# Fetching one of 32 gathered row blocks by single-row transfers from SyncE

## What is computed

```python
def _gcn_layer(x, W, b, edge_weight, edge_src, edge_dst):
    support = x @ W
    msgs = support[edge_src] * edge_weight[:, None]
    agg = jax.ops.segment_sum(msgs, edge_dst, num_segments=N_NODES)
    return agg + b
h = jax.nn.elu(_gcn_layer(x, W1, b1, edge_weight, edge_src, edge_dst))
h = jax.nn.elu(_gcn_layer(h, W2, b2, edge_weight, edge_src, edge_dst))
```

## Time and profile before

| | us |
|---|---|
| median of 3 runs (5253.92 to 5268.12) | 5263.27 |
| the profiled execution | 5257.51 |
| its span, first to last instruction | 5255.6 |

### The profile page before, as it was taken

How to read it: one execution, slowest core, us unless ns; L and a number is a source line. 1 busy time by engine, 2 the same in 40 slices (tenths; PEclk the granted TensorE clock), 3 DMA queues, 4 the chain that set the end, 5 groups by cost and what they waited for, 6 DMA issues and landing times. The chain is left out here.

```text
span 5255.6 us, 89454 instructions
## 1 busy us (share of the span) xinstructions
PE 4074.3 (78%) x25266; PEld 3747.3 (71%) x25267; DVE 2650.4 (50%) x9578; ACT 814.5 (15%) x2507; POOL 3445.0 (66%) x3639
## 2 busy tenths in 40 slices
PE   0577777777777777769988999898989987069998
PEld 0467666666667776758888888888888886058886
DVE  7433333333333333355676666767666666234444
ACT  2001111111111111111222222222222222011111
POOL 0577777777777777757777777777777774632222
PEclk9867777777777777778999999999999998589999
DMA  7444444444444444434555454555545553632221
GB/s 212 142 128 132 130 132 132 130 132 130 132 131 133 132 130 132 129 89 125 147 147 152 143 151 145 147 149 146 151 144 148 147 146 109 188 112 70 67 70 65
DMA packets 409075, 693.81 MB, mean 132 GB/s; under 512 B 108237, under 2 KB 275661, under 8 KB 408893
## 3 DMA queue, kind: packets, MB, share of 16 engines
q0 software_dynamic: 177312, 488.43, 32.8%
q1 hardware_dynamic: 195765, 163.17, 10.6%
q10 hardware_dynamic: 35920, 41.25, 2.2%
HBM read 562.84 MB, written 129.68 MB: 132 GB/s over the span
## 5 line engine op out<-in xcount | busy, mean ns | idle before, releaser
L395 PEld LDWEIGHTS sums<-sel,rows 128*128 128x128 f32 x13312 | 1888.7, 222 | 768.0 <-DMA rows<-xn,idx 440.8
L395 PE MATMUL sums<-sel,rows 128*128 128x64 f32 x13312 | 1894.5, 305 | 672.9 <-DMA rows<-xn,idx 354.6
L451 POOL DMA_INDIRECT rows<-xn,idx x1664 | 1577.8, 948 | 642.4 <-issue 630.8
L451 POOL DMA_INDIRECT rows<-h,idx x1664 | 1585.3, 953 | 578.5 <-issue 528.9
L403 DVE TENSOR_SCALAR sel<-cols,rel_now,wgt_now 128x64 f32<-128x64 f32 x3360 | 780.4, 336 | 7.8
L409 DVE TENSOR_TENSOR agg<-agg,sums 128x128 f32 x832 | 240.3, 289 | 783.9 <-issue 604.7
L603 DVE TENSOR_TENSOR pre<-z,b_g 128x256 f32<-128x256 f32 x98 | 41.6, 424 | 526.8 <-PE z L598 526.8
L1807 PE MATMUL y_ps<-w,e_hidden 128*128 128x256 f32 x1248 | 286.1, 389 | 0.0
L1795 PE MATMUL e_hidden_ps<-tokens_t,w 128*128 128x256 f32 x1248 | 279.2, 381 | 4.4 <-DVE e_hidden L1864 3.6
L983 PE MATMUL hidden_ps<-xt,w 128*128 128x128 f32 x1664 | 265.2, 282 | 17.2 <-ACT msg_t L1104 17.0
L1735 POOL DMA_INDIRECT out<-y_result,target_i x80 | 79.5, 994 | 291.3 <-DVE y_result L1849 271.3
(11 more groups left out here) (211 smaller groups left out, 4547.4 us busy)
## 6 DMA issues: line engine op xcount, KB each, us to landing
xe<-zeros ACTq DMA_DIRECT2D x104, 258.0 KB, 4.1
rows<-xn,idx POOLq DMA_INDIRECT x1664
rows<-h,idx POOLq DMA_INDIRECT x1664
w<-in_ffn_w POOLq DMA_DIRECT2D x16, 1024.0 KB
tile<-xn SPq DMA_DIRECT2D x105, 128.0 KB
ln_rows<-in_x SPq DMA_DIRECT2D x52, 256.0 KB
xn<-ln_normed ACTq DMA_DIRECT2D x52, 256.0 KB, 4.4
kv_tile<-xn SPq DMA_DIRECT2D x104, 128.0 KB
```

Of the source, the lines that this page charges most:

```text
L395: last = nc.tensor.matmul(sums[:, g, h, :], rows[:, u, k, h * P:(h + 1) * P], sel[:, u, k, :], start=(c == 0), stop=(c == GROUP - 1))
L451: nc.gpsimd.indirect_dma_start(out=rows[:, u, k, :], out_offset=None, in_=source, in_offset=bass.IndirectOffsetOnAxis(ap=idx[:, u, k:k + 1 ...
```

## The change

In layer 1 alone (`by_row=True`), row block 15 of turn `(i, 1)` is no longer gathered by POOL. SP fetches its 128 rows with 128 plain transfers of 1 KB. The row numbers come from a new input `in_src_rows`, one row block a line; SP loads one line into `near_idx`, reads 16 numbers at a time into registers, and issues 16 transfers with these as addresses. The first 64 rows are issued in SP's body for `u` = 0, the other 64 in its body for `u` = 1, each behind that body's wait for the landed row blocks and its `idx` load, and ahead of its `kv_tile` load. PE waits for all 128 (`near_loaded`) ahead of the last group of turn `(i, 1)`.

In layer 2 (`by_row=False`) the store of the attention's result moves: SP's body for a turn stores the tile of one turn earlier, and waits for that store to land after the other stores and loads of the body, not ahead of them. The table `upto` is made in `route`, where it is used, and no longer in `prepare`; this frees its room.

```diff
+NEAR = 16
+HALF_ROWS = P // 2
...
+def load_rows(nc, engine, of, most):
+
+    values = nc.values_load_multi_w_load_instructions(of, engines=(engine,))[1]
+    return [value.with_bounds(min_val=0, max_val=most) for value in values]
...
+        near_idx = sb("near_idx", [1, P], I32) if by_row else None
+        far = [SLOTS, SLOTS - 1 if by_row else SLOTS]
+        last_bank = [16 * (far[u] - GROUP * SUB) for u in range(2)]
...
+                def near_rows(j, u):
+
+                    if u == 0:
+                        sp.wait_ge(rows_used[1], j + 1)
+                        wait_apart(sp, near_idx_loaded, 16 * j + 16, m.sp_passed)
+                    for k in range(u * HALF_ROWS, (u + 1) * HALF_ROWS, NEAR):
+                        ids = load_rows(nc, mybir.EngineType.SP, near_idx[0:1, k:k + NEAR], N - 1)
+                        for n in range(NEAR):
+                            sp.dma_start(rows[k + n:k + n + 1, 1, SLOTS - 1, :], source[bass.ds(ids[n], 1), :]
+                                         ).then_inc(near_loaded, 16)
+                    if u == 1:
+                        at = j * (2 * SLOTS) + (3 * SLOTS + far[1])
+                        sp.dma_start(near_idx[:, :], m.in_src_rows[bass.ds(at, 1), :]).then_inc(near_idx_loaded, 16)
+
                 def turn(i, u):
-                    sp.wait_ge(rows_loaded[u][BANKS - 1], 16 * GROUP * SUB * i)
+                    sp.wait_ge(rows_loaded[u][BANKS - 1], last_bank[u] * i)
                     sp.dma_start(idx[:, u, :], m.in_src[bass.ds(2 * i + u, 1)].rearrange("o p c -> (o p) c")
                                  ).then_inc(idx_loaded[u], 16)
+                    if by_row:
+                        near_rows(i - 1, u)
                     mix.free(sp, i - 1, u)
                     mix.load(sp, 2 * i + u, u)
                     mix.store(sp, i - 1, u)
                     dense.sp(sp, i - 1, u)
+                    mix.release(sp, i - 1, u)
...
-                        for k in range(SLOTS):
+                        for k in range(far[u]):
...
+                        if by_row and u == 1 and g == TURN - 1:
+                            wait_apart(pe, near_loaded, 16 * P * (i + 1), m.pe_passed)
                         last = window_products(g, u, rows_used[1 - u] if g == 0 else None)
...
+    def store(sp, i, u):
+
+        if not before_first(i, u, 1):
+            store_tile(sp, *behind(i, u))
+
+    def release(sp, i, u):
+        if not before_first(i, u, 1):
+            free_result(sp, *behind(i, u))
```

More of the change, by code:

```diff
@@ L233, in _ @@
                                         base=0, pattern=[[-1, P]], channel_multiplier=1).then_inc(iotas_done, 1)
-                nc.gpsimd.affine_select(out=m.upto[:, :], in_=m.ones[:, :], compare_op=ALU.is_ge, fill=0.0,
-                                        base=0, pattern=[[1, P]], channel_multiplier=-1).then_inc(iotas_done, 1)
                 pool.wait_ge(spans_done, 2)
@@ L305, in _ @@
                 normalise(loops - 1, PSLOTS - 1, False)
-                dve.wait_ge(iotas_done, 4)
+                dve.wait_ge(iotas_done, 3)
                 nc.vector.tensor_copy(m.cols[:, :], iota_i[:, :]).then_inc(tables_done, 1)
@@ L339, in _, with gather @@
                 dve.wait_ge(tables_done, 15)
-def gather(nc, m, layer, source, mixer, denser):
+def gather(nc, m, layer, source, mixer, denser, by_row):
     with ExitStack() as ctx:
@@ L370, in gather @@
         sums = ps("sums", TURN * KD, WIN).rearrange("p (g k) w -> p g k w", g=TURN)
+        near_idx = sb("near_idx", [1, P], I32) if by_row else None
+        far = [SLOTS, SLOTS - 1 if by_row else SLOTS]
+        last_bank = [16 * (far[u] - GROUP * SUB) for u in range(2)]
         idx_loaded = [sem(f"idx_loaded{u}_") for u in range(2)]
+        near_idx_loaded = sem("near_idx_loaded")
+        near_loaded = sem("near_loaded")
         rows_loaded = [[sem(f"rows_loaded{u}{b}_") for b in range(BANKS)] for u in range(2)]
@@ L416, in _ @@
                     mix.load(sp, u, u)
+                if by_row:
+                    sp.dma_start(near_idx[:, :], m.in_src_rows[SLOTS + far[1]:SLOTS + SLOTS, :]).then_inc(near_idx_loaded, 16)
                 mix.load_weights(sp)
                 dense.load_weights(sp)
+                def near_rows(j, u):
[10 more added lines that the diff above has]
+                        sp.dma_start(near_idx[:, :], m.in_src_rows[bass.ds(at, 1), :]).then_inc(near_idx_loaded, 16)
                 def turn(i, u):
-                    sp.wait_ge(rows_loaded[u][BANKS - 1], 16 * GROUP * SUB * i)
+                    sp.wait_ge(rows_loaded[u][BANKS - 1], last_bank[u] * i)
                     sp.dma_start(idx[:, u, :], m.in_src[bass.ds(2 * i + u, 1)].rearrange("o p c -> (o p) c")
                                  ).then_inc(idx_loaded[u], 16)
+                    if by_row:
+                        near_rows(i - 1, u)
                     mix.free(sp, i - 1, u)
@@ L434, in _ @@
                         turn(i, u)
+                if by_row:
+                    for u in range(2):
+                        near_rows(loops - 1, u)
+                    wait_apart(sp, near_idx_loaded, 16 * loops + 16, m.sp_passed)
                 mix.load_past(sp)
                 for u in range(2):
+                    mix.store(sp, loops - 1, u)
                     dense.sp(sp, loops - 1, u)
+                    mix.release(sp, loops - 1, u)
                 mix.stored(sp)
@@ L546, in turn @@
                         if g % SUB == 0:
-                            pe.wait_ge(rows_loaded[u][g // SUB], 16 * GROUP * SUB * (i + 1))
+                            pe.wait_ge(rows_loaded[u][g // SUB],
+                                       (16 * GROUP * SUB if g < TURN - SUB else last_bank[u]) * (i + 1))
+                        if by_row and u == 1 and g == TURN - 1:
+                            wait_apart(pe, near_loaded, 16 * P * (i + 1), m.pe_passed)
                         last = window_products(g, u, rows_used[1 - u] if g == 0 else None)
@@ L834, in keys_values @@
     mix.dve, mix.act, mix.after = dve, act, after
-    mix.store = lambda sp, i, u: None
+    mix.store = mix.release = lambda sp, i, u: None
     mix.load_weights = load_weights
@@ L911, in free, with behind, store_tile @@
         sp.wait_ge(base_ready, 2 * i + (u + 1))
-    def store(sp, i, u):
+    def behind(i, u):
+        return (i, 0) if u else (i - 1, 1)
+    def store_tile(sp, i, u):
         t = 2 * i + u
@@ L916, in store, with free_result @@
         sp.dma_start(m.mix[bass.ds(t * P, P), :], result[:, u, :]).then_inc(stored[u], 16)
+    def free_result(sp, i, u):
         sp.wait_ge(stored[u], 16 * i + 16)
         sp.sem_inc(result_free[u], 1)
+    def store(sp, i, u):
[4 more added lines that the diff above has]
+            free_result(sp, *behind(i, u))
     def load_past(sp):
@@ L925, in all_stored @@
     def all_stored(sp):
-        for u in range(2):
-            store(sp, TURNS // 2 - 1, u)
+        store_tile(sp, TURNS // 2 - 1, 1)
+        free_result(sp, TURNS // 2 - 1, 1)
     def turn_tile(pe, t, u, i):
@@ L1111, in act_end @@
         guess_sd(act, TURNS - 1, 1)
-    mix.load, mix.free, mix.store, mix.stored = load, free, store, all_stored
+    mix.load, mix.free, mix.store, mix.release, mix.stored = load, free, store, release, all_stored
     mix.pe_begin, mix.pe, mix.pe_end = pe_begin, pe, pe_end
@@ L1461, in route @@
         spare_f = sb("spare_f", [P, NT])
+        upto = sb("upto", [P, P])
         blocks_i = sb("blocks_i", [1, NE], I32)
@@ L1483, in _ @@
             def _(pool):
+                nc.gpsimd.affine_select(out=upto[:, :], in_=m.ones[:, :], compare_op=ALU.is_ge, fill=0.0,
+                                        base=0, pattern=[[1, P]], channel_multiplier=-1).then_inc(iotas, 1)
                 nc.gpsimd.iota(left_i[:, :], [[-1, NE]], base=NE, channel_multiplier=0).then_inc(iotas, 1)
@@ L1496, in _ @@
                     half = chosen[:, k * HALF:(k + 1) * HALF, :]
-                    nc.tensor.matmul(nth_ps[k], m.upto[:, :], half, start=True, stop=True)
+                    nc.tensor.matmul(nth_ps[k], upto[:, :], half, start=True, stop=True)
                     nc.tensor.matmul(count_ps[k], m.ones[:, :], half, start=True, stop=True).then_inc(counted, 1)
@@ L1513, in _ @@
                                         ALU.subtract).then_inc(shifted, 1)
-                dve.wait_ge(iotas, 2)
+                dve.wait_ge(iotas, 3)
                 nc.vector.tensor_copy(left_f[:, :], left_i[:, :])
@@ L1896, in program @@
     m = Memory()
-    (m.x, m.in_src, m.in_dst, m.in_dst_rows, m.in_wgt, m.in_w_g1, m.in_b_g1, m.in_w_g2, m.in_b_g2,
+    (m.x, m.in_src, m.in_src_rows, m.in_dst, m.in_dst_rows, m.in_wgt, m.in_w_g1, m.in_b_g1, m.in_w_g2, m.in_b_g2,
      m.in_w_q, m.in_w_k, m.in_w_v, m.in_w_m, m.in_w_1, m.in_w_2, m.in_ln1_g, m.in_ln1_b, m.in_ln2_g, m.in_ln2_b,
@@ L1927, in program @@
         m.ident = sb("ident", [P, P])
-        m.upto = sb("upto", [P, P])
```

(5 more changed lines are left out.)

## The result

The changed kernel takes 7,249.32 us, median of 4 runs (7,248.49 to 7,260.83); the kernel before, on the same chip, 5,259.25 us (5,253.92 to 5,268.12). The ratio is 1.379, 95% interval 1.376 to 1.381. The profiled execution has a span of 7,247.0 us.

What follows compares the result with a forecast made beforehand. POOL's gathers were taken to set layer 1's pace, 40.0 us a pair; SP's chain of 62.4, 9.1 and 1.8 us makes 73.3. The 33.3 us difference times 52, 1,732 us, added to 5257.5 gives 6,990 us, range 6,000 to 7,750.

Steps and rivals of the forecast that it cites:

- the chain on SP: Layer 1: SP's in-order instructions for both halves and what follows them set the pair's time, 73.3 us.
- PE's wait: Layer 1, PE ahead of the products at line 395: idle some 30 us in every second turn, ended by a `rows` transfer.
- POOL's gap: Layer 1, between POOL's gathers: grows from 0.30 us to some 33 us once a pair.
- layer 1's stretch of gathers: Layer 1's part of the span: grows from some 2,080 to some 3,800 us.
- The row: SP, one row's transfer: 0.26 us of issue and 0.19 us of instructions around it, 0.45 us; ends 0.19 and 0.70.
- The register load: SP, loading 16 row numbers into registers: 0.6 us with its gaps, ends 0.4 and 1.7; four per half.
- From the second half to the next first half: SP, last issue to next first load: landing 2.0, group 3 2.0, sums 0.3, `h` 3.8, loop end and `idx` 1.0; 9.1 us.
- Between the halves: SP's issues of `kv_tile`, `h` and `idx` with their gaps between the two halves: 1.8 us.
- The sum: Layer 1, a pair's time: two halves 62.4 us, plus 9.1 and 1.8 us, together 73.3 us against 40.0 before.
- The first rival: Layer 1: SP keeps up if a half takes under 11.65 us, 0.145 us a row; kernel faster, 5,192 us; chance 0.04.
- The second: Rival on SP: a one-piece issue costs 0.06 us, 0.25 us a row; 400 us more, 5,660 us; chance 0.14.
- The third: Rival on SP's queue: rows served one after another, 2.0 us each; pair 272 us, kernel 17,300 us; chance 0.03.

Runs made afterwards that it cites:

- run with the spare buffer: Changed kernel with all 128 row transfers sent to a spare buffer, PE not waiting for them, an added SP wait for their landing: 6,862.7 us, ratio 1.305.

## Why the prediction was right, point by point

The direction, the chain on SP and the stage held, and 7,249 us lies in the range; the 6,990 us forecast is 259 us short. What the prediction gave as signs all came out larger: PE's wait is 42.7 us a pair (some 30 forecast), POOL's gap 40.5 us (some 33), and layer 1's stretch of gathers 4,039 us (some 3,800). Term by term:

- **The row: 0.45 us forecast, 0.41 measured.** The issue is 0.228 us (0.26 forecast), what stands around it 0.18 (0.19). Extrapolating from 256 and 128 pieces was good to 0.03 us.
- **The register load: 0.6 us forecast, 1.23 measured.** Sixteen values take over three times the one value of the earlier trace rows, and the load stood inside the ends 0.4 and 1.7. Per half the two errors cancel: 31.2 us forecast, 31.87 measured. The half was right partly by luck.
- **From the second half to the next first half: 9.1 us forecast, 12.9 measured.** This is the term that was mis-sized. The landing was shorter, 1.2 us after the last issue. Group 3 took 3.65 us, not 1.90 as in the earlier trace rows, at a granted clock of 0.50, the lower level (1.2 GHz), after PE had idled 42 us; the forecast took a duration from a busy stretch for a place behind a stall, although has such a place too, 3.68 us behind 4.68 us of idle time, at a granted clock of 0.50 as well. And 3.3 us pass between the end of the issue of `h` (2043.46) and `idx` (2046.76), where the forecast had 1.0 us for the loop's end and `idx` together; nearly all of it is a pause behind the loop's branch (last section).
- **Between the halves: 1.8 forecast, 2.24 measured.**
- **The sum:** 31.87 + 31.86 + 12.9 + 2.24 = 78.9 us a pair in place of 73.3. Over the 40.0 us of before that is 38.9, times the 51 full periods between the first and the last pair 1,982 us; layer 2 starts 1,984.5 us later. That these agree so closely is chance in part: the first four periods, whose pairs are unrolled ahead of the loop, are only some 73.5 us, and at the end 70.8 us lie between layer 1's last gather and layer 2's first, where it was 33.2. The loss lies in layer 1 as forecast; layer 2's 6 us stay under the 80 us that would have spoken against the reasons.
- **The first rival** (SP keeps up) wanted 0.145 us a row. Half that dose of rows, placed late, passed POOL by 22 us a pair, and even bare issues at 0.295 us were too slow.
- **The second** (0.06 us for the issue, 0.25 us a row) is refuted by the issue itself, 0.228 us; what stands around it, 0.18 us, is as it had it. The run with fixed addresses comes near its 0.25 us and 5,660 us (0.295 us, 5,792 us) by another way: there the issue is 0.252 us, and hardly anything stands around it.
- **The third** (2.0 us a row in series) is refuted: rows follow at 0.41 us and PE starts 1.2 us after the last issue, so a row's landing overlaps the next issues. Queue q1 has 13,418 packets more than before, some two a row: in the trace one of 1,024 bytes and one of 4. So a row goes as one packet of data; on which DMA engine is not shown, so it stays open whether all rows share one. The rule of the Trainium skill against small transfers (DMA: Bandwidth & Descriptors, section Rules for kernel authors) agrees with the direction; here the price was the issuing engine's instructions, not the transfers.

One step of the mechanism was wrong, though the sum did not use it. The prediction has the second half begin when the 15 gathers of its turn have landed. In the kernel after, SP's `idx` load ahead of it goes out some 19 us after the last of them has ended on POOL, since the first half takes longer than those gathers. So PE stands through the end of the first half too, which is how its wait became 42.7 us; the wait for the landed row blocks decides in the run with the late half alone.

One thing the prediction did not separate: its chain goes through group 3 and PE's wait for the rows. The run with the spare buffer shows that SP's queue alone, without that wait, costs 1,606 us.

## What to carry to other kernels

Before work is moved to an "idle" queue, multiply its instructions by the time of one there, and compare with the period of the loop, not with the queue's busy share: 128 small issues with addresses from registers were 64 us in a loop of 40. List what stands behind them in that in-order queue, since those loads stall even if nobody waits for the moved work. And measure what the relieved engine really saves: a gather of 80 rows cost 96% of one of 128.

## What the hardware showed that was not expected

- **SP pauses behind the branch of a long loop body.** In the three kernels whose SP body has 423 to 425 recorded instructions a pass (the changed kernel, all rows early, the spare buffer) the last issue of a pass and the first of the next are 2.9 to 3.4 us apart (medians). With 159 to 227 instructions (half early, half late, fixed addresses) it is 0.6 to 0.7 us. In the pass shown above, the branch at line 463 starts at 2043.6 us and the next instruction at 2046.5, with nothing between. Over the layer these gaps are 2.4 to 3.7 us in the three kernels and 0.2 to 0.3 us in the three others, in the one with 48 rows (177 instructions) and in the kernel before (25). Behind the last branch of the changed kernel's loop, which is not taken, it is 0.05 us. In the three kernels a packet of the instruction queue is moved within the gap at each of the 45 taken branches, in the others at none; that queue has 285 packets there, 45 to 49 in the others, 38 before. The Trainium skill, Advanced Engine Details and Errata, section ISA Cache, gives two lines of 256 instructions to an engine; a body of 423 can lie over three lines, so that agrees. That SP waits for these packets fits all of this; no run changed the fetch alone.
- **The same gathers land later in one run than in another.** In the kernel before, SP's `idx` load, which waits for a turn's row blocks, goes out 1.9 to 2.0 us after the last gather of that turn has ended on POOL, as the forecast's 2.0 us has it. In the run with the late half it is 2.1 to 4.2 us (median 2.7), 3.8 us in the pass shown (2009.48 and 0.95 us, then 2014.19). SP stands ready for it each time, and POOL goes on with the next turn's gathers in both kernels. Why the landing differs is open.
- **An issue with a fixed address takes longer, 0.252 us against 0.228,** though the row as a whole is cheaper. No run here tells why.
